# One run of small float32 products per round in a delta-rule block, its first two normed rows both on VectorE, and the weight products moved out of the first stage

## What is computed

```python
def delta(x):                        # LayerNorm of x goes in
    q, k, v = split(x @ gates_w + gates_b, 3)
    k = k / norm(k)
    A = tril(k @ k.T, -1) + eye(512)
    u = solve_triangular(A, v, lower=True)
    return ((q @ k.T) @ ((x @ lr_w + lr_b) * u)) @ out_w + out_b
x0 = layernorm(x)
x1 = x0 + delta(LN(x0)); x2 = x1 + relu(LN(x1) @ w1 + b1) @ w2 + b2      # LN with gain and shift
x  = x + x2
out = x + (silu(n @ wg.T) * (n @ wu.T)) @ wd.T,   n = layernorm(x)      # int weights / 127
```

## Time and profile before

| what | value |
|---|---|
| median of 3 runs | 1553.88 us (1553.77 to 1553.95) |
| the profiled execution: its own time | 1553.63 us |
| its span in the profile | 1551.9 us |
| PE busy | 1533.4 us, 99% of the span |
| PE weight loads (PEld) | 1362.1 us, 88% |
| DVE, ACT, POOL busy | 74%, 55%, 49% |
| granted TensorE clock | full speed over the span |

### The profile page before, as it was taken

How to read it: one execution, slowest core, us unless ns; L and a number is a source line. 1 busy time by engine, 2 the same in 40 slices (tenths; PEclk the granted TensorE clock), 3 DMA queues, 4 the chain that set the end, 5 groups by cost and what they waited for, 6 DMA issues and landing times.

```text
span 1551.9 us, 30623 instructions
## 1 busy us (share of the span) xinstructions
PE 1533.4 (99%) x10840; PEld 1362.1 (88%) x10840; DVE 1151.1 (74%) x3075; ACT 856.0 (55%) x1692; POOL 767.0 (49%) x886
## 2 busy tenths in 40 slices
PE   8999999899999999999999999999999999999998
PEld 7999998788888888888888888888888888888887
DVE  7777884578877777788777777887777777777774
ACT  6877775355555555555555555555555555555553
POOL 5456872245444454444444544444444444444442
PEclk9999999999999999999999999999999999999999
DMA  7999998212222322222222222222222222222200
GB/s 247 347 312 321 323 335 259 62 62 76 76 76 75 116 76 76 76 75 74 70 73 106 81 74 76 75 76 76 75 100 78 76 76 75 76 75 75 73 17 28
DMA packets 150169, 178.24 MB, mean 115 GB/s; under 512 B 78850, under 2 KB 132098, under 8 KB 141826
## 3 DMA queue, kind: packets, MB, share of 16 engines
q1 hardware_dynamic: 150018, 176.28, 34.4%
HBM read 98.64 MB, written 77.59 MB: 114 GB/s over the span
## 4 chain that ended last, share of the span: by engine, by line
PE 80%; DVE 2%; ACT 1%; issue 0%; POOL 0%; DVEq 0%; ACTq 0%
PE ps L175 34%; PE ps L1142 23%; PE ps L1152 12%; PE ps L1073 4%; PE ps L1045 4%; PE ps L1062 2%; PE ps L1051 1%; PE ps L258 0%; PE ps L1183 0%; DVE xh3T_lo L1542 0%; DVE xinv L1487 0%; DVE low L199 0%; PE ps L1169 0%; DVE bt_lo L1542 0%; POOL gl_lo L1743 0%
## 5 line engine op out<-in xcount | busy, mean ns | idle before, releaser
L1767 POOL TENSOR_TENSOR hl<-late,hh 128x512 fp32r<-128x512 f32 x128 | 166.4, 1300 | 209.8 <-ACT hh L1347 209.8
L1342 ACT ACTIVATE late<-ps 128x512 f32<-128x512 f32 x192 | 114.3, 595 | 171.0 <-PE ps L1142 171.0
L1537 DVE TENSOR_TENSOR late<-ps,late 128x512 f32<-128x512 f32 x192 | 132.7, 691 | 94.9 <-PE ps L1142 93.1
L1152 PE MATMUL ps<-wdT,hh 128*128 128x256 f32 x744 | 199.8, 304 | 0.0
L1152 PE MATMUL ps<-wdT,hl 128*128 128x256 f32 x744 | 182.7, 281 | 0.3 <-DVE hl L1542 0.3
L1347 ACT ACTIVATE hh<-late 128x512 fp32r<-128x512 f32 x192 | 120.8, 629 | 108.7 <-DVE late L1537 108.7
L1714 POOL TENSOR_TENSOR sc<-ls,mhalf 128x4 f32<-128x4 f32 x64 | 65.7, 1026 | 221.4 <-DVE ls L1504 221.4
L1142 PE MATMUL ps<-xh3T_hi,wgT 128*128 128x512 f32 x384 | 153.7, 400 | 1.1 <-DVE xh3T_lo L1542 1.1
L1142 PE MATMUL ps<-xh3T_lo,wuT 128*128 128x512 f32 x384 | 151.9, 395 | 0.0
L1142 PE MATMUL ps<-xh3T_lo,wgT 128*128 128x512 f32 x384 | 151.8, 395 | 0.0
L1142 PE MATMUL ps<-xh3T_hi,wuT 128*128 128x512 f32 x384 | 151.5, 395 | 0.0
(11 more groups left out here) (220 smaller groups left out, 4730.8 us busy)
## 6 DMA issues: line engine op xcount, KB each, us to landing
xhT_scratch<-xhTk SPq DMA_DIRECT2D x32, 1024.0 KB, 6.7
xhT<-xhT_scratch SPq DMA_DIRECT2D x32, 1024.0 KB, 6.4
gg_scratch<-late SPq DMA_DIRECT2D x32, 640.0 KB, 4.1
gg<-gg_scratch SPq DMA_DIRECT2D x32, 640.0 KB, 3.9
xk<-in_L_attn_x_dram SPq DMA_DIRECT2D x32, 512.0 KB, 5.5
xt<-in_L_attn_x_dram SPq DMA_DIRECT2D x32, 512.0 KB, 4.1
out_dram<-late SPq DMA_DIRECT2D x31, 512.0 KB, 2.9
low_scratch<-late SPq DMA_DIRECT2D x128, 16.0 KB, 2.9
```

The lines of the kernel that those rows point to most:

```text
L1152: mm = pe.matmul(ps[:, (FG, FU)[j // 2], (j % 2) * C:(j % 2 + 1) * C], part[:, h, blk(j)], wdT[:, h, :], start=(h == 0 and part is hh), st ...
L1342: act.activation(sg[:, h % 2, :], ps[:, FG, :], ACT.Silu, scale=QUANT).then_inc(sg_ev[h], 1)
L1537: dve.tensor_tensor(hf[:, h % 2, :], ps[:, up_bank(h), :], sg[:, h % 2, :], ALU.mult).then_inc(hf_ev[h], 1)
L1767: pool.tensor_tensor(hl[:, h, :], hf[:, h % 2, :], hh[:, h, :].bitcast(F32), ALU.subtract).then_inc(hl_ev[h], 1)
```

## The change

1. PE, full rounds: the first piece of `pe_down` for token block 0 is cut from five hidden blocks to four. Row block 1 is issued directly behind it, then the transposes of x2, then row block 2, with nothing between them. The rest of `pe_down` for token blocks 0 and 1 follows, in an order that takes hidden blocks 4 and 5 last. Token block 0 goes to bank A2, block 1 to FG, blocks 2 and 3 to FU.
2. DVE: in full rounds `masked` is first, then normed blocks 0 and 1, row block 1, `dve_hl(4)` (which left the end of the round before), `dve_lo` of half 0, `dve_hl(5)`, `dve_lo` of half 1, row block 2.
3. POOL: its normed block 0 is gone, in all rounds.
4. The two weight products leave the first stage. `pe_factors` makes them in round 0 in place of 14 `keep_busy` products (16 float32 matmuls), ACT and DVE split the result (`act_factors`, `dve_factors`). `a0` and `xa` hold the operands and are allocated ahead of both stages.

```diff
@@ pe_body
                     if down:
                         after(pe, sg_ev[HB - 1], i - 1)
-                        pe_down(pe, i, 0, range(HB - 1))
+                        after(pe, a0_ev[TB - 1], i)
+                        pe_down(pe, i, 0, range(HB - 2 if att else HB - 1))
+                    if att and down:
+                        pe_row_block(pe, i, 1)
...
                     if mlp:
-                        pe.wait_ge(xh2_first, i)
                         pe.wait_ge(xh2_done, i)
                         pe.wait_ge(xh2_rest, i)
...
                         pe_transposes(pe, (FO0, FO1), xn, t2_ps)
                     if att and down:
-                        pe_row_block(pe, i, 1)
-                    if down:
+                        pe_row_block(pe, i, 2)
+                        pe_down(pe, i, 1, range(HB - 2))
+                        for h in (HB - 2, HB - 1):
+                            pe_down(pe, i, 0, (h,))
+                            pe_down(pe, i, 1, (h,))
+                    if down and not att:
                         pe_down(pe, i, 0, (HB - 1,))
                         pe_down(pe, i, 1)
-                    if att and down:
-                        pe_row_block(pe, i, 2)
                     if att and not down:
                         pe_row_block(pe, i, 3)
                         pe_weights(pe, i, 3)
-                        if i == 0:
-                            keep_busy(pe, S0, 4)
+                        pe_factors(pe, i, wvT, wo, range(2))
...
+                    if att:
+                        after(pe, ot_ev[0], i - 1)
                         pe_bt(pe, i, 3)
...
+                        pe.wait_ge(factor_done, 1)
                         pe_square(pe, A0, bt2, wvo2, e_ps)
@@ dve_body
+                    if att and down:
+                        masked(dve, i)
                     if mlp:
...
-                        dve.tensor_scalar(xn[:, 1, :], a0[:, 1, :], mv2[:, 1, 0:1], sc2[:, 0, 1:2],
-                                          ALU.subtract, ALU.mult).then_inc(xh2_first, 1)
-                    if att and down:
-                        masked(dve, i)
-                    if down:
+                        for j in range(2):
+                            op = dve.tensor_scalar(xn[:, j, :], a0[:, j, :], mv2[:, j, 0:1], sc2[:, 0, j:j + 1],
+                                                   ALU.subtract, ALU.mult)
+                        op.then_inc(xh2_done, 1)
+                    if att:
+                        row_block(dve, i, 1 if down else 2)
+                    if down and att:
+                        dve_hl(dve, i - 1, HB - 2)
+                        dve_lo(dve, xh2T2[1], xh2T2[0], (FO0, FO1), t2_hi, t2_ev, i, (0,))
                         dve_hl(dve, i - 1, HB - 1)
-                    if att:
-                        row_block(dve, i, 1 if down else 2)
-                    if mlp:
+                        dve_lo(dve, xh2T2[1], xh2T2[0], (FO0, FO1), t2_hi, t2_ev, i, (1,))
...
+                        dve_factors(dve, i, wvo2[1][:, :, :], wvo2[0][:, :, :], 1)
...
                     if mlp:
                         dve_up(dve, i, 4)
                         dve_up(dve, i, 5)
-                        dve_hl(dve, i, 4)
+                        if i == NS - 1 or not att:
+                            dve_hl(dve, i, 4)
@@ pool_body
-                        for k in range(CB):
-                            after(pool, t3_ps[k], i - 1)
-                        pool.wait_ge(ln2_done, i)
-                        pool.tensor_scalar(xn[:, 0, :], a0[:, 0, :], sc2[:, 0, 0:1], sc2[:, 1, 0:1],
-                                           ALU.mult, ALU.add).then_inc(xh2_done, 1)
@@ prep_pe (first stage)
-                if q == 4:
-                    pe.wait_ge(tq_done, 2)
...
-                                mm = pe.matmul(piece(2 * m + h), wvT[:, k, m * P:(m + 1) * P], wo[:, k, h * P:(h + 1) * P],
-                                               start=(k == 0), stop=(k == CB - 1))
-                    mm.then_inc(vo_ps, 1)
-                if q == 5:
...
@@ new
+                def pe_factors(pe, i, lhs, rhs, quarters, last=False):
+
+                    if i > 0:
+                        return
+                    for q in quarters:
+                        m, h = q // 2, q % 2
+                        for k in range(CB):
+                            mm = pe.matmul(ps[:, S0, q * P:(q + 1) * P], lhs[:, k, m * P:(m + 1) * P],
+                                           rhs[:, k, h * P:(h + 1) * P], start=(k == 0), stop=(k == CB - 1))
+                    if last:
+                        mm.then_inc(factor_ps, 1)
```

More of the change, by code:

```diff
@@ L116, in delta_block_kernel @@
         wvo2 = pair("wvo", [P, CB, C])
+        a0 = sb("a0", [P, TB, C])
+        xa = sb("xa", [P, TB, C])
+        wkT, wqT, wvT, wo = a0[:, 0:CB, :], a0[:, CB:2 * CB, :], xa[:, 0:CB, :], xa[:, CB:2 * CB, :]
         w12 = pair("w1", [P, CB, C])
@@ L749, in delta_block_kernel @@
             LOADS = 11
-            whole = ((w2f, w22, None, 0), (w1f, w12, w1_done, CB), (wqk, wqk2, qk_done, 1), (wvo, wvo2, vo_done, 1))
+            whole = ((w2f, w22, None, 0), (w1f, w12, w1_done, CB))
             PREP = 8
-            SPLIT_AT = 6
+            PREP_PS = 4
+            SPLIT_AT = 4
             def piece(q):
@@ L882, in prep_evicted @@
             def prep_evicted(pe, q):
-                if 0 <= q < SPLIT_AT:
-                    done, count = ((w_shift_done, 1), (b1_sb, 1), (tq_done, 1), (tq_done, 2), (vo_done, 1), (qk_done, 1))[q]
+                if 0 <= q < PREP_PS:
+                    done, count = ((w_shift_done, 1), (b1_sb, 1), (tq_done, 1), (tq_done, 2))[q]
                     pe.wait_ge(done, count)
             def prep_pe(pe, q):
-                if 0 <= q < SPLIT_AT:
+                if 0 <= q < PREP_PS:
                     pe.wait_ge(xhT_lo[1], q + PREP + 2)
@@ L1151, in pe_down @@
                                 pe.wait_ge(made[h], i - 1)
-                            mm = pe.matmul(ps[:, (FG, FU)[j // 2], (j % 2) * C:(j % 2 + 1) * C], part[:, h, blk(j)],
+                            bank, c0 = DOWN[j]
+                            mm = pe.matmul(ps[:, bank, c0:c0 + C], part[:, h, blk(j)],
                                            wdT[:, h, :], start=(h == 0 and part is hh),
@@ L1253, in pe_body @@
                         pe_weights(pe, i, 4)
-                        if i == 0:
-                            keep_busy(pe, S0, 2)
+                        pe_factors(pe, i, wvT, wo, range(2, 4), last=True)
                     if down:
@@ L1266, in pe_body @@
                         if i == 0:
-                            keep_busy(pe, S0, 2)
+                            pe.wait_ge(factor_done, 1)
+                        pe_factors(pe, i, wkT, wqT, range(1))
                     if mlp:
@@ L1274, in pe_body @@
                         pe_weights(pe, i, 6)
-                        if i == 0:
-                            keep_busy(pe, S0, 2)
+                        pe_factors(pe, i, wkT, wqT, range(1, 2))
                     if down:
@@ L1298, in pe_body @@
                         pe_weights(pe, i, 8)
-                    if i == 0:
-                        keep_busy(pe, S0, 4)
+                        pe_factors(pe, i, wkT, wqT, range(2, 4), last=True)
                     if mlp:
@@ L1347, in act_hh, with act_factors @@
                     act.activation(hh[:, h, :], hf[:, h % 2, :], ACT.Copy).then_inc(hh_ev[h], 1)
+                def act_factors(act, i, dst, n):
+                    if i == 0:
+                        act.wait_ge(factor_ps, n)
+                        act.activation(flat(dst), ps[:, S0, :], ACT.Copy).then_inc(factor_hi, 1)
                 def act_z(act, i, j):
@@ L1556, in dve_lo, with dve_factors @@
                         dve_rest(dve, lo[:, k, :], ps[:, banks[k], :], hi[:, k, :], hi_done[k], n, done[k])
+                def dve_factors(dve, i, lo, hi, n):
+                    if i == 0:
+                        dve.wait_ge(factor_hi, n)
+                        dve.tensor_tensor(lo, bank3(S0), hi.bitcast(F32), ALU.subtract).then_inc(factor_done, 1)
                 def dve_out(dve, i, half):
@@ L1563, in dve_out @@
                     if i <= NS:
-                        down = ps[:, (FG, FU)[half], :].rearrange("p (j c) -> p j c", c=C)
+                        down = bank3(FU) if half else ps[:, A2:FG + 1:FG - A2, 0:C]
                     else:
```

45 lines of the change are left out of this document (16 added, 29 removed).

## The result

The changed kernel takes **1573.24 us** (median of 4 runs, 1572.44 to 1573.86) against 1553.91 for the kernel before beside it: a ratio of 1.0121, 95% interval 1.0108 to 1.0135. It is slower, as forecast, but by 19.3 us where 7.8 were worked out, and it lies outside the range. The profiled execution took 1573.86 us, its span is 1572.1.

The account below looks back on a forecast made before the run. PE, busy in 99% of the span, was taken as the bound. -3.6 + 1.6 + 0.2 + 30 x (0.02 + 0.25) + 6 x 0.25 = +7.8 on 1553.63, with the median 0.25 higher: 1561.7 us; range 1550.0 to 1567.2.

Parts of the forecast that it names:

- the two terms of the stage boundary: Weight products moved: -3.6 us for leaving the first stage, 0 for coming back in round 0.
- The first stage's gain (-3.6): Rounds 12 and 13: the weight products' sixteen float32 matmuls and their switches leave PE's queue, -3.6 us.
- rival 3: First stage: its gain isn't there, as another engine or the loads set its pace; +3.6, 1565.3 us; chance 0.08.
- The wait before line 1046: Full rounds: PE's product reading row block 3's copies waits 0.25 us, bounds 0 and 0.45.
- The held cast: Full rounds: VectorE's `gl_hi` is held until GpSimd's `xa2` ends, then runs, ending 0.41 us later.
- PE needs `hl` 5 near 847.8, in time: Full round 15: VectorE's `hl` of block 5 ends at 847.62, so PE does not wait for it.
- Eaten by the mask: Full rounds: single run saves 0.15 us, transposes behind mask and both normed rows lose 0.18; net +0.02 to +0.03.
- The memset: Six full rounds: GpSimd's 0.96 us memset between `xa2` and `gl_lo` delays VectorE's next subtraction; 0.25 us each.
- rival 2: Six full rounds: the memset gets in ahead of the held cast, row block 3 0.9 later; +5.4, 1567.1 us; chance 0.08.
- Round 1: `xa2` starts early on GpSimd and holds both normed rows on VectorE, so PE's transposes start later: +1.6 us.
- The rival without a hold: Cast and normed rows not held, GpSimd and VectorE take turns: -2.5, 1551.4 us; chance 0.24.
- the reading as half speed: Cast beside `xa2`: both go on at half speed, cast ends by 850.2; sum as in The rival without a hold.

Follow-up runs that it names:

- the second experiment: Kernel before, with one added wait making `xa2` in full rounds also wait for the first half of `xh2T_lo`: 1569.49 us, ratio 1.0094.
- the kernel with eleven products: Changed kernel with eleven `keep_busy` products in place of five at the end of the first stage: 1572.05 us, ratio 1.0110.
- the first experiment: Changed kernel with VectorE's `hl` of block 5 moved directly behind `hl` of block 4, ahead of `xh2T_lo`'s first half: 1554.98 us, ratio 1.0004.
- the first three experiments: Changed kernel with `hl` 5 earlier: 1554.98 us; kernel before with `xa2` made late: 1569.49; changed kernel with cast `gl_hi` on ScalarE: 1560.62.

## Why the prediction was wrong

The sum was +7.8 and the two spans differ by 20.2. Of the 12.4 us between, 7.8 lie in the thirty full rounds (+17.4 measured, +9.6 worked out), 4.4 between the start and the end of round 0 (+0.8 in place of -3.6), and 0.2 behind that. So the steps that failed are the size of PE's wait in a full round and the two terms of the stage boundary.

- **The first stage's gain (-3.6) was there, and half of it did not arrive.** The transposes of rounds 12 to 14 are as close as worked out. But the first level product comes only 1.8 earlier. ScalarE and VectorE now wait for the DMA `gg_scratch`, as shown above, and by the waits view of the DMA queue SyncE's wait for the load of `xt` grows from 1.9 to 3.9. I read from this that transfers end the stage, rival 3 at a place where I did not look: it was argued away by the rounds in the middle. The trace of the second experiment, whose first stage is that of before, has the `gg_scratch` rows as well, with 4.4 and 4.2 us, and its level product comes at 258.70, no later than before: the transfers were just in time there, and PE's shorter work laid them bare. No run changed the transfers, so this is a reading. In the eight kernels with this move the first level product came at 255.7 to 257.9.
- **PE's idle time at the boundary was not priced.** The granted clock fell after PE's longer idle time there, which cost 2.6 in round 0; the kernel with eleven products has 30.50 there where the clock stayed full. Of the two terms I summed to -3.6, +0.8 was left in the profiled execution. With eleven products the clock stayed full in the profiled executions of two kernels out of three, and with five in one of the five that have this move.
- **A full round: +0.27 was forecast, +0.52 came.** The wait before line 1046 was worked out as 0.25 and measured 0.45, and a second wait, 0.12, was put at nothing. The held cast was right in kind: it ends 0.42 after `xa2`, where 0.41 was worked out. Three things were mis-sized. The first half of `xh2T_lo` starts 0.73 after `hl` of block 4 (856.47 against 855.74) and not 0.60; with it `xa2` starts 5.16 after the level product and not 5.07, takes 2.44, and the cast ends 0.14 later than worked out. PE's product starts 0.15 after the last copy (861.87, then 862.02) and not 0.05. Together with the 0.25, less 0.03 by which PE itself is later, that is the 0.45. And the step "PE needs `hl` 5 near 847.8, in time" was false by 0.1: `hl` 5 ended 4.99 after the level product, not 4.89, and PE waits for it, 0.12 over the rounds.
- **The rows on VectorE.** The transposes come 2.13 after the level product, forecast 2.21; the mask starts 0.04 after the level product ends, not 0.12. With both waits gone and GpSimd's row back, a full round is 0.18 shorter than before, where 0.15 was worked out for the single run. The two rows one behind the other give 0.12 of that back. "Eaten by the mask" said too much: -0.06 was left, as the first experiment shows.
- **The memset** was counted in six rounds for 0.25 each, its place in the queue left to rival 2. That mechanism is what happened, at 0.9 each, in two rounds. That 1.5 us were forecast and 1.8 came is luck.
- **Round 1: +1.6 forecast, +1.56 came**, by the mechanism named. **The end: +0.2 forecast, +0.9 came**: 0.5 of it is round 31, which is a full one and was counted there. In round 32 PE waits 0.27 for the rows, and its transposes start 0.16 later behind `pe_down` than before; 0.3 lies behind PE's last product, and what makes it was not followed up.

The rival without a hold is excluded: casts of 1.39 to 2.33 us, and what the first three experiments did to the time, speak against it. The Trainium skill has the rule that decides it, on another page than the one the prediction weighed: SBUF — State Buffer, section "SBUF: two separate sides", says that GpSimd and VectorE, when VectorE is in a two-port mode or has two SBUF inputs, share a pair of ports under an exclusive lock, held by whichever starts first for its whole instruction, and not a split of bandwidth. The casts that end 0.41 to 0.43 after `xa2` or the memset agree; the reading as half speed, which the prediction set beside its own, does not. One row differs from "whichever starts first": in round 8 the cast was there 0.95 us before the memset and still came after it, and there the measurement decides.

## What to carry to other kernels

When an instruction is moved on one engine, follow what it releases on the others to their ends: here a subtraction that came 1.95 us later released a GpSimd addition that then lay over a VectorE cast two steps away. That overlap, put alone into the kernel before, costs 15 us, and PE's wait for the subtraction itself another 3.6 (30 times 0.12). Put VectorE's casts, its normed rows and its subtractions of two SBUF inputs where GpSimd is idle, and what it copies out of PSUM beside GpSimd. A stage's pace in the middle says nothing of its end: before time is booked from a stage, look at what ends it, and what the engine does until the next begins.

## What the runs showed of the hardware beyond that

- A GpSimd instruction issued right behind a running one goes ahead of a VectorE cast that has already waited for 0.95 us; and a memset, which reads nothing, holds it as well (2.33 us for a cast of 0.56).
- Not everything on VectorE is held. The four 32x64 copies out of PSUM take 0.93 us under `xa2` (858.39 in round 15) and 0.93 without it in the kernel before; the batch-norm statistics of a 128x256 block in SBUF take 0.41 us free and 0.42 beside GpSimd. The subtraction `h_lo` of two SBUF inputs takes 0.69 free, 1.33 under `gl_lo`, and 2.25 where the memset had made `gl_lo` late.
- The granted clock after an idle stretch of PE ahead of the first level product, in the ten profiled executions: full after 1.29, 1.32, 1.43, 1.44 and 2.42 us, fallen after 1.89, 1.93, 2.49, 2.97 and 2.99 us. The length of the gap alone does not decide it. Where it fell, round 0 was 1.5 to 2.6 us longer than 30.5.
- PE's four 32-column products of row block 1 are followed by the transposes after 0.22 us in most rounds of the kernel with the row on GpSimd, but after 0.37 in rounds 15 and 19, where both rows had been ready just as early (in round 15 the transposes start at 841.90, row 1 was done at 841.53). What sets this was not found.
